# Last layer, first pass: the rows of a tile's destination range come from DRAM through the queue, and TensorE reads them at a fixed address

## What is computed

```python
msg_s = (s_n @ Ws_src)[src] + (s_n @ Ws_dst)[dst]
msg_v = einsum(v_n, Wv_src)[src] + einsum(v_n, Wv_dst)[dst]
w1 = rbf @ W_rbf
m1_s, m1_v = _cg_tp(msg_s, msg_v, y0, y1, w1[...])   # products with the edge's y
a = leaky(m1_s @ W_alpha) ...                        # scores of 4 heads
val_s, val_v = m1 @ W_val, gated by a sigmoid
m2_s, m2_v = _cg_tp(val_s, val_v, y0, y1, w2...)
h = m2 @ W_vlin                                      # one row of 160 per edge
```

## Time and profile before

| | |
|---|---|
| median of 3 runs | 7282.01 us (7276.09 to 7289.44) |
| the profiled execution | 7280.35 us, span 7278.6 us |
| TensorE busy, loads of weights | 93%, 62% of the span |
| VectorE busy | 86% |
| GpSimd busy | 68% |
| ScalarE busy | 52% |
| HBM read, written | 469.60 MB, 300.92 MB |

### The profile page before, as it was taken

One profiled execution on the slowest core, in us unless ns is written; L12 is line 12 of the kernel. 1 busy time (PEld: TensorE's weight loads), 2 busy tenths in 40 slices (PEclk: granted clock), 3 DMA queues, 4 the chain that ended last, 5 costly groups with the idle time before them and its releaser, 6 DMA issues. The chain is left out here.

```text
span 7278.6 us, 114637 instructions
## 1 busy us (share of the span) xinstructions
PE 6735.4 (93%) x33428; PEld 4526.3 (62%) x33428; DVE 6241.9 (86%) x17139; ACT 3802.7 (52%) x10244; POOL 4946.0 (68%) x3534
## 2 busy tenths in 40 slices
PE   6999999997899999989999983999999999998488
PEld 3445444444555555645555551888888888887376
DVE  6999999996698888778888872999999999998794
ACT  3555455553333333433333331777777777776485
POOL 2887888884377777547777734888888888885000
PEclk7999999997799999989999995999999999999797
DMA  8999999998222222112222212444444444443363
GB/s 230 175 176 177 174 178 175 175 177 188 70 65 64 65 66 65 48 51 68 68 69 69 69 35 67 90 96 98 98 95 95 96 94 97 94 97 75 100 192 97
DMA packets 551879, 778.19 MB, mean 107 GB/s; under 512 B 94113, under 2 KB 402630, under 8 KB 551014
## 3 DMA queue, kind: packets, MB, share of 16 engines
q0 software_dynamic: 323136, 419.33, 34.7%
q1 hardware_dynamic: 223894, 350.90, 15.9%
q10 hardware_dynamic: 4240, 0.64, 0.1%
HBM read 469.60 MB, written 300.92 MB: 106 GB/s over the span
## 5 line engine op out<-in xcount | busy, mean ns | idle before, releaser
L678 POOL DMA_INDIRECT fore<-node_table,src_i x1664 | 1714.5, 1030 | 647.1 <-issue 501.1
L1629 DVE TENSOR_TENSOR work<-work 128x384 f32<-128x384 f32 (+5 forms) x4912 | 1998.1, 433 | 54.1 <-DMA work<-src_sum 26.7
L792 POOL DMA_INDIRECT fore<-src_table,put_i x784 | 1592.4, 2031 | 242.4 <-issue 234.4
L745 POOL DMA_INDIRECT src_sum<-work,put_i x808 | 1294.6, 1602 | 396.4 <-issue 174.5
L1381 PE MATMUL bank<-work 128*128 128x384 f32 (+1 forms) x3328 | 1201.3, 504 | 14.4 <-DVE work L1629 14.4
L1381 PEld LDWEIGHTS bank<-work 128*128 128x128 f32 x3328 | 604.2, 191 | 693.4 <-issue 311.4
L951 ACT ACTIVATE work<-bank 64x512 f32<-64x512 f32 x416 | 245.8, 591 | 1434.7 <-PE bank L1348 1434.6
L1629 DVE TENSOR_TENSOR work<-work,bank 128x384 f32 (+6 forms) x2068 | 891.6, 431 | 80.2 <-issue 70.5
L1333 PE MATMUL bank<-work 128*128 128x480 f32 x1616 | 750.3, 598 | 2.2 <-DVE work L1629 1.9
L1362 PEld LDWEIGHTS bank<-w_fc,work 64*128 64x128 f32 x3328 | 532.7, 188 | 238.1 <-issue 225.9
L1479 PE MATMUL bank<-ident,work 128*128 128x128 f32 x4704 | 650.8, 275 | 26.6 <-DVE work L1629 25.1
(11 more groups left out here) (274 smaller groups left out, 12744.4 us busy)
## 6 DMA issues: line engine op xcount, KB each, us to landing
edge_h<-work SPq DMA_DIRECT2D x196, 320.0 KB
work<-edge_h SPq DMA_DIRECT2D x196, 320.0 KB, 3.4
work<-keys SPq DMA_DIRECT2D x196, 256.0 KB, 6.2
fore<-in_dst_row SPq DMA_DIRECT2D x196, 256.0 KB, 4.3
fore<-node_table,src_i POOLq DMA_INDIRECT x1664, 2.7
work<-in_edge_attr SPq DMA_DIRECT2D x196, 128.0 KB, 6.1
src_sum<-work SPq DMA_DIRECT2D x4, 6240.0 KB, 37.6
work<-src_sum SPq DMA_DIRECT2D x100, 240.0 KB, 4.3
```

The costliest lines, as they stand in the source:

```text
L678: return pool.indirect_dma_start(dst, None, table, bass.IndirectOffsetOnAxis(ap=idx, axis=0), bounds_check=bound, oob_is_err=True)
L745: pool.indirect_dma_start(src_sum[t], bass.IndirectOffsetOnAxis(ap=put_i[:, e:e + 1], axis=0), E.run[:, g % 2, t * 480:(t + 1) * 480], Non ...
L792: pool.indirect_dma_start(T.rows[:, b, t, :], None, src_table, bass.IndirectOffsetOnAxis(ap=put_i[:, e:e + 1], axis=0), compute_op=ALU.add ...
L1629: return V_.tensor_tensor(o, p, q, op)
```

## The change

SyncE loads, for each of the first three tiles of a group, the 128 rows of the tile's window from `dst_table` in DRAM into a buffer of two groups, `T.ranges`, at an address that it takes from registers, twelve of which it loads every four groups. TensorE no longer loads the numbers and no longer computes addresses; it waits for the three loads and reads the buffer. The buffer takes 960 floats of each partition of `work`; what follows it moves up.

```diff
@@ semaphores
-            "turns_out", "gd_out", ..., "dst_turned", "dst_rows_mm",
+            "turns_out", "gd_out", ..., "dst_turned", "dst_rows_mm", "ranges_in0", "ranges_in1",
@@ l3_views
             v.cv = g(2, GROUP, 196)
+            v.ranges = g(2, 3, DIM)
             at_f = g.used()
@@ SyncE
+                range_of = [sp.alloc_register(f"sp_range{i}") for i in range(12)]
+
+                def ranges(g):
+                    b = g % 2
+                    if g % 4 == 0:
+                        sp.load(range_of[0:12], tile_window_i[0:1, 0:TILES].rearrange("p (g t) -> p g t", t=GROUP)[:, g:g + 4, 0:3])
+                    if g >= 2:
+
+                        sp.wait_ge(s.dst_rows_mm, 2 * g - 2)
+                    for t in range(3):
+                        window = sp.snap(range_of[g % 4 * 3 + t], min_val=0, max_val=WINDOWS - 1)
+                        sp.dma_start(T.ranges[:, b, t, :], dst_table.rearrange("(j p) c -> j p c", p=P)[bass.ds(window, 1)]
+                                     .rearrange("o p c -> (o p) c")).then_inc(s.ranges_in1 if b else s.ranges_in0, 16)
...
                 for g in range(2):
                     dst_keys(g)
                     rbf(g)
+                    ranges(g)
...
-                unrolled(GROUPS, [(0, lambda g: rbf(g) if g >= 2 else None), (-2, lambda g: dst_keys(g) if g >= 2 else None), (5, keep_h)])
+                unrolled(GROUPS, [(0, lambda g: rbf(g) if g >= 2 else None), (-2, lambda g: dst_keys(g) if g >= 2 else None),
+                                  (-2, lambda g: ranges(g) if g >= 2 else None), (5, keep_h)])
@@ TensorE, dst_rows
                     g, at = h // 2, h % 2 * 2
-                    if h % 8 == 0:
-                        n = min(16, TILES - 2 * h)
-                        pe.load(held[0:n], tile_window_i[0:1, 2 * h:2 * h + n])
                     if at == 0:
+
+                        pe.wait_ge(s.ranges_in1 if g % 2 else s.ranges_in0, 48 * (g // 2 + 1))
 
                         pe.wait_ge(s.dst_turned, g + 1)
...
                     for t in range(2):
-                        window = pe.snap(held[(2 * h + t) % 16], min_val=0, max_val=WINDOWS - 1)
-                        last = nc.tensor.matmul(gd[:, t * DIM:(t + 1) * DIM], T.turned[:, g % 2, at + t, :],
-                                                skip[:, bass.ds(window, 1), 0:DIM].rearrange("p o c -> p (o c)"),
+                        last = nc.tensor.matmul(gd[:, t * DIM:(t + 1) * DIM], T.turned[:, g % 2, at + t, :], T.ranges[:, g % 2, at + t, :],
                                                 start=True, stop=True)
```

More of the change, by code:

```diff
@@ L248, in build @@
             "h_done", "h_kept0", "h_kept1",
-            "turns_out", "gd_out", "fourth_in0", "fourth_in1", "border_src_in", "border_rows", "border_kept", "dst_keys_in0", "dst_keys_in1", "dst_turned", "dst_rows_mm",
+            "turns_out", "gd_out", "fourth_in0", "fourth_in1", "border_src_in", "border_rows", "border_kept", "dst_keys_in0", "dst_keys_in1", "dst_turned", "dst_rows_mm", "ranges_in0", "ranges_in1",
             "scores_turned", "scores_in_sbuf", "scan_ready", "scan_turned", "scan_free", "scores_shifted")}
```

## The result

The changed kernel took 7294.63 us (median of 20 runs, 7270.40 to 7311.08), the kernel before 7281.20 us beside it (20 runs). The ratio is 1.0017, interval 1.0009 to 1.0025: slower by 13 us, with an interval of 7 to 18 us; the middle lies just under the 0.2% (14.6 us) that the prediction took as the bound of what can be told, the interval reaches over it. The forecast was 7285 us, 3 us more than before: the time is inside its range, the change is over four times its size. The profiled execution took 7294.74 us with a span of 7293.0, 14.4 us above the span before. Of the experiments, e5, e6, e7 and e9 ran in a series in which all executions were slower, the kernel before at 7679.13 us, so of these four the ratio counts, and the pace inside the pass, which doesn't differ.

What follows compares the result with a forecast made beforehand. TensorE sets the pace early, GpSimd late. 187 groups at 10.98 us give +5.6, the first ten or so give back 3: +3 on 7280.35, 7283; the median stands 1.7 higher, 7285 us; range 7245 to 7325, its own 7278 to 7296.

Steps and rivals of the forecast that it cites:

- the late state comes at once: Pass: GpSimd's gathers set the pace from some group under 20; 187 groups at 10.98 us, +5.6, sum +3; 0.56.
- Only where VectorE pauses: Third gather of a group: GpSimd gets in only where VectorE waits for TensorE; out at 5.45 us, otherwise 6.74.
- Register work leaves TensorE: TensorE before L1507: saves 0.12 + 0.53 / 4 = 0.25 us a group while TensorE sets the pace, otherwise nothing.
- The other term, 0.53 / 4: TensorE's halves with a register load: 0.53 us more to be had, once every four groups.
- the first rival: TensorE's time is won, the early TensorE-set pace lasts: 7266 us, or 7211 if throughout; chance 0.22.
- The reason for the tipping: VectorE's slack against TensorE falls from 0.21 to 0.09 us, so two gathers in a row are shut out every four groups.
- late `m1`: Early part, every fourth group: VectorE's `m1` starts some 0.25 us late for no recorded cause, eating the 0.21 us slack.
- Traffic at 0: DMA: range loads add 384 packets, 1.9 us of every engine per group; cost 0, ends 0 and 1.9 us a group.
- the rival: Range loads delay the fourth gather's landing: 0.16 us a group, 30 us, 7315; if half meet, 60 us; chance 0.22.
- The added wait on TensorE: TensorE before the turned keys: range loads issued by about offset 2.3 (one group in four 3.5), landed by 7; cost nothing.
- SyncE's wait: SyncE waits until both halves of group g - 2 are read, ahead of `keep_h`, `rbf` and next keys; cost nothing.
- the hole does not close: TensorE before L1507: fixed addresses may leave a pause; changes nothing in the GpSimd-paced state, 7285 us; no chance given.

Runs made afterwards that it cites:

- e5: Changed kernel, VectorE waiting for its own last product of `m1` before `m2` in the first twelve groups only; ratio 0.9952.
- e6: Kernel before, VectorE waiting for its own last product of `m1` before `m2` in every group; ratio 0.9963.
- e7: Changed kernel, VectorE waiting for its own last result at the end of every group, between `edge_out` and the key comparisons; ratio 1.0008.
- e9: Changed kernel, VectorE waiting for its own result between the first and second operation of `m2` in every group; ratio 0.9940.
- e1: Changed kernel, VectorE waiting for its own last product of `m1` before the first product of `m2` in every group; 7234.73 us, ratio 0.9930.
- e8: Kernel e1, with `dst_rows` ahead of `edge_w3` on TensorE; 7327.57 us, ratio 1.0056.
- e11: Changed kernel, TensorE loading registers and reading at their address as before in the first five groups only; 7286.08 us against 7288.40, ratio 0.9994.
- e10: Changed kernel, twelve more already fulfilled waits of VectorE before its first comparison of the pass; 7289.69 us against 7288.40, ratio 0.9999.
- e2: Kernel before, TensorE always reading window 0 at a fixed address, without register loads, address work or range loads; 7291.33 us, ratio 1.0010.
- e3: Changed kernel, TensorE loading registers and reading `skip` as before; the range loads run but nobody reads them; 7285.99 us, ratio 1.0002.
- e4: Changed kernel, TensorE still loading 16 registers every eighth half, which no instruction reads; 7286.80 us, ratio 1.0003.

## Why the prediction was right, and where it was not

*The forecast, "the late state comes at once": right.* Product at 3.96, gather at 6.74, VectorE waiting for the gather in every group (80.0 us in all), 10.98 us a group: as written. (Of the 80.0 us some 17, 0.35 in every fourth group, are VectorE's own late start.) The price, 187 groups at 10.98 = 2053.3 us, measured 2055.0. That a pause of VectorE at the right place lets a waiting gather out 0.8 to 1.3 us earlier is shown by e1, e9 and e7. "Only where VectorE pauses" is too strong: the gather at 5513.00 took 1.66 us beside VectorE's products without a pause. The one at offset 3.7, beside such products too, takes 3.05 us, and the one that starts at 5511.16, in VectorE's idle time before `m1`, 1.54. What makes these differ no run shows.

*"Register work leaves TensorE", 0.12 us per plain two-tile half: mis-sized, measured 0.* I read the pause of 0.28 us in the row of the weight loads as an idle engine. It was the next load's wait while matmuls of 224 columns ran (e8). The other term, 0.53 / 4, was right: 24.1 us between e6 and e1. TensorE's period is thus 10.69, not 10.57; the first rival at its best ("throughout, 187 x 10.57 = 1976.6") could only have been 1998.9, which is what e1 runs.

*The reason for the tipping: right in kind, off in its numbers.* With TensorE at 10.69 the slack of VectorE stays 0.21, not 0.09. I had the late state begin at "some group under 20" and give back 3 us before that; it began at group 2, and the first seven groups gave back 1.2. What I hadn't seen is the start: it was TensorE's own wait for registers in group 1 that opened the early state (e11). So "at once" was in part luck: the reason given, a slack that shrinks, was false, and the reason that holds, a start without that wait, stands nowhere in the prediction. What the prediction does carry is that without the register wait a late `m1` isn't made good; by that alone the state would have come at group 19 (e11), still under its 20. That the register wait of every fourth group also kept it alive, as argued from the earlier trace rows, fits e11 (18 groups) against before (67).

The late `m1` itself, there "for no recorded cause", is tied to the place of VectorE's instructions (e5, e10).

*Why "+3" became 14.4.* The size was not forecast: 3 us against 14.4 in the profiled executions and 13 in the medians. In parts: the early pace before was 10.83, not 10.89; my window of the earlier trace rows didn't begin and end on an `m1`, which hid some 4 us; the late pace after, + 1.7; the first groups 1.8 less than hoped; start and end of the pass 1.1 + 3.2, which I had at 0. Each is small, and the sum stays within "its own range is 7278 to 7296", at its upper end.

*Traffic at 0: right* (e2 and e3). The queue's share rose by 9.2 points where 384 x 79 ns had given 17: the packets that came on top, some 430 a group (50512 over the 1290 us) and not 384, took 38 ns each, half that average. The fourth gather's last mark came at 1.85 us after its end, against 1.83 before (medians, groups 90 to 193): 0.02 us, where the rival had 0.16. That packets of the loads and of the gather meet at all was an assumption; whether they do, no run shows. *The added wait on TensorE: right.* In three groups of four the three loads are issued by offset 2.7 at most in the median, near the 2.3 forecast. In the fourth, the one shown, they are issued from 4.0 to 5.4, where 3.5 was forecast: SyncE's load of 12 registers took 2.70 us (median of 49) and not the 1.10 taken over from TensorE. The last of them lands at offset 7.2 in the median even so (6.0 to 6.6 in the three others), and TensorE waits for a range load only in the start-up (three times, 90.9 us, the longest 74.3; before, it stood 77.28 us for VectorE at that place). *SyncE's wait: nothing, as forecast.*

*The last rival, "the hole does not close": it came true*, and in the late state it changed nothing, as written.

## What to carry to other kernels

Before removing work from an engine, find out which engine sets the pace in each stretch, and whether the stall that you remove is where another engine gets its turn: here a wait of 0.53 us every four groups held open the door for GpSimd, and a pause of 0.14 us per group, put in on purpose, brought 0.7%. The pause of 0.28 us between weight loads was no idle TensorE here (in e1 the matmuls behind it stood still for 0.3 us in all 187 groups); read the matmuls' row beside such a pause before costing it. A change in the number of instructions moves the place of all that come behind it; here that alone, at e5, took 0.35 us out of every fourth group, so a control should keep the count. And measure a pace from the start of a group to the start of a group, with the state read from the trace, since kernels in different states had times within 0.1%.

## What was unexpected of the hardware

- Two steady states of one instruction stream: the third gather out at 5.5 or at 6.74 us, 10.69 or 10.9 to 10.98 us a group, decided by 0.04 to 0.14 us of idle time in VectorE's stream while a gather waits (e9, e1). One `m1` that started 3.65 us after its gather's end in place of 2 turned the one into the other for the 156 groups that were left (e5).
- A register load of 1.1 us costs TensorE 0.46 us where its next instructions need the values (e6), and nothing where no instruction does (e4). SyncE's load of 12 registers took 2.70 us.
- A wait of 1.13 us of TensorE was followed by a granted clock of 0.72 over 6 us, in which it made 24 matmuls in place of 34; four kernels of four with such a wait (1.11 to 1.31 us), none of nine without it at that place.
- VectorE starts 0.35 us late once in 128 instructions: 0.40 us after its wait is over and not 0.04, in 44 of 44 cases. Twelve instructions more ahead of the pass's later groups took it away (e5: 10.905 against 10.98 us a group), six took it away too, but then a gather landed 0.35 us late (e10). A packet of 8192 bytes on the instruction queue moves along: at offset 1.3 to 2.1 in the changed kernel, 6.2 to 6.9 in e5, 9.3 to 10.1 in e10.
